# Opening of a four-layer graph network on one core: how bucket totals, walk tables, records and low weights are made

## What is computed

```python
edge_index = jnp.stack([src, dst])
x = _layernorm(x + _L0_gnn_ref(x, edge_attr_128, src, dst, L0_gnn_W0, ...), axis=-1)
x = _layernorm(x + _L1_gnn_ref(x, edge_index, L1_gnn_W1, ...), axis=-1)
x = _layernorm(x + _L2_gnn_ref(x, edge_index, L2_gnn_W1l, ...), axis=-1)
x = _layernorm(x + _L3_gnn_ref(x, edge_index, L3_gnn_W, L3_gnn_b), axis=-1)
```

```python
h = jnp.concatenate([n_embed[senders], n_embed[receivers]], axis=-1)
h = jnp.tanh(h @ W0 + b0)
h = jnp.tanh(h @ W1 + b1)
h = h @ W2 + b2
h = h * (e_embed @ Wg)
return _segment_mean(h, senders, n_embed.shape[0])
```

## Time and profile before

| | |
|---|---|
| runs | 3201.62, 3200.44, 3201.49 us; median 3201.49 |
| the profiled execution | 3200.9 us, its span 3199.2 us |
| busy, share of the span | PE 96%, weight loads 78%, VectorE 70%, ScalarE 49%, GpSimd 44% |
| opening | from 0 to about 106 us of the span |
| products of the totals (line 234) | 13 groups of 32 |
| 40 slices, granted clock | full in nearly all; 0.9 in the second |

### The profile page before, as it was taken

One profiled execution on the slowest core, in us unless ns is written; L12 is line 12 of the kernel. 1 busy time (PEld: TensorE's weight loads), 2 busy tenths in 40 slices (PEclk: granted clock), 3 DMA queues, 4 the chain that ended last, 5 costly groups with the idle time before them and its releaser, 6 DMA issues. The chain is left out here.

```text
span 3199.2 us, 65986 instructions
## 1 busy us (share of the span) xinstructions
PE 3084.0 (96%) x17656; PEld 2507.0 (78%) x17658; DVE 2244.3 (70%) x5604; ACT 1566.8 (49%) x3155; POOL 1395.0 (44%) x1479
## 2 busy tenths in 40 slices
PE   7699999999999999999998989999999999999899
PEld 6588888888888888888886777777777888887666
DVE  7688888888888888888886989995655222245532
ACT  2366666666666666666663777771111111001354
POOL 2577777777777777777773222220000000000111
PEclk9899999999999999999998999999999999999999
DMA  4555555555555555555554888887566777678475
GB/s 160 162 166 161 164 163 163 164 164 160 162 164 164 164 163 165 162 164 164 161 162 130 252 253 258 266 266 236 166 183 187 231 219 223 220 231 264 90 121 95
DMA packets 298303, 584.86 MB, mean 183 GB/s; under 512 B 43362, under 2 KB 150843, under 8 KB 298235
## 3 DMA queue, kind: packets, MB, share of 16 engines
q1 hardware_dynamic: 180960, 280.20, 29.5%
q0 software_dynamic: 90416, 254.46, 28.8%
q10 hardware_dynamic: 26858, 49.32, 4.2%
HBM read 493.97 MB, written 110.32 MB: 189 GB/s over the span
## 5 line engine op out<-in xcount | busy, mean ns | idle before, releaser
L967 PE MATMUL bank<-parts,ring 128*128 128x512 f32 x2500 | 622.8, 398 | 4.7 <-DVE T_buf L1739 2.6
L967 PEld LDWEIGHTS bank<-parts,ring 128*128 128x128 f32 x2500 | 461.0, 188 | 105.6 <-issue 5.7
L612 POOL DMA_INDIRECT msgs<-rows_out,sidx x416 | 409.1, 983 | 151.9 <-issue 95.1
L605 POOL DMA_INDIRECT p_in<-p_tab,gidx x416 | 404.6, 973 | 139.6 <-issue 122.7
L605 POOL DMA_INDIRECT q_in<-q_tab,gidx x416 | 399.0, 959 | 126.7 <-issue 125.2
L667 PE MATMUL bank<-hidden1h,w1h 128*108 128x512 f32 x936 | 407.1, 435 | 2.1 <-DVE hidden2l L855 2.1
L667 PE MATMUL bank<-w2h,hidden2h 108*128 108x256 f32 x1248 | 403.4, 323 | 0.0
L668 PE MATMUL bank<-hidden1l,w1h 128*108 128x512 f32 x936 | 369.0, 394 | 0.0
L669 PE MATMUL bank<-hidden1h,w1l 128*108 128x512 f32 x936 | 367.7, 393 | 0.0
L1123 PE MATMUL bank<-at_dst,at_src 128*128 128x320 f32 x1088 | 329.5, 384 | 36.3 <-DVE at_src L1083 29.1
L774 ACT ACTIVATE hidden2h<-bank,b1c 108x512 fp32r<-108x512 f32 (+1 forms) x312 | 214.8, 689 | 297.0 <-PE bank L683 297.0
(11 more groups left out here) (252 smaller groups left out, 6058.4 us busy)
## 6 DMA issues: line engine op xcount, KB each, us to landing
ring<-counts SPq DMA_DIRECT2D x500, 320.0 KB, 3.4
R_buf<-msgs SPq DMA_DIRECT2D x544, 130.0 KB, 3.1
counts<-cells ACTq DMA_DIRECT2D x125, 320.0 KB, 3.4
eT<-in_edge_T SPq DMA_DIRECT2D x104, 256.0 KB, 2.9
R_buf<-counts POOLq DMA_DIRECT2D x25, 480.0 KB, 5.2
R_buf<-counts POOLq DMA_DIRECT2D x25, 320.0 KB, 5.6
p_in<-p_tab,gidx POOLq DMA_INDIRECT x416, 3.2
q_in<-q_tab,gidx POOLq DMA_INDIRECT x416, 3.2
```

What stands on the lines that cost most here:

```text
L605: pool.indirect_dma_start(out=rows_in[:, z, c], out_offset=None, in_=tab[:], in_offset=bass.IndirectOffsetOnAxis(ap=gidx[:, z, which, c:c ...
L612: pool.indirect_dma_start(out=msgs[:], in_=rows_out[:, z, c], in_offset=None, out_offset=bass.IndirectOffsetOnAxis(ap=sidx[:, z, c:c + 1], ...
L967: mm = pe.matmul(bU[t].rearrange("p (w c) -> p w c", w=2), ring[:, cell(odd, a), t * P:(t + 1) * P].bitcast(dt), parts[k % 2][:, :, a].bit ...
```

## The change

Five edits, all in the opening.

1. **Totals over four chunks at once.** One product takes the one-hots of four chunks as its stationary side (4 x 25 = 100 columns) and those of the same four as its moving side (4 x 5 = 20). Of the 100 by 20 sums only the four 25 by 5 blocks of equal chunks are wanted; `found` and `spread` become 100 partitions high, and the identity that `spread` is multiplied by keeps only those blocks. The sum over partitions behind tile 17 reads 100 rows instead of 25.
2. **Walk tables from bf16.** `ended`, `jumpT` and `sign` are bf16, and `ones_b` takes the place of `ones_f`.
3. **Records piecewise.** The five instructions of `record()` stand singly behind `q_out` of tiles 5, 7, 9, 11 and 13.
4. **Low weights on GpSimd.** A third of `w1l` and of `w2l` each behind `xl` of tiles 8, 9 and 10.
5. The remainder of `w1h` stays on VectorE, behind `q_out` of tile 15.

```diff
@@ totals (PE) @@
-                            for c in range(OB):
-                                at = c % GC * B
-                                mm = pe.matmul(psum[7][0:T, at:at + B], oh_s[:, slot, c], oh_d[:, slot, c],
+                            for c in range(0, OB, GC):
+                                four = slice(c, c + GC)
+                                mm = pe.matmul(psum[7][0:GC * T, 0:GC * B],
+                                               oh_s[:, slot, four].rearrange("p c a -> p (c a)"),
+                                               oh_d[:, slot, four].rearrange("p c b -> p (c b)"),
                                                start=(n == 0 and slot == 0 and c == 0),
-                                               stop=(n == HN - 1 and slot >= 2 and c >= OB - GC),
+                                               stop=(n == HN - 1 and slot >= 2 and c == OB - GC),
@@ table (PE) and its operands @@
-                        lhs = [ones_f[0:BK - 1, :], jumpT[0:BK, 0:1], sign[0:BK - 1, 0:1]][what]
+                        lhs = [ones_b[0:BK - 1, :], jumpT[0:BK, 0:1], sign[0:BK - 1, 0:1]][what]
...
+                jumpT = ssb("jumpT", [P, P], BF16)
+                sign = ssb("sign", [P, 1], BF16)
+                ended = ssb("ended", [P, NST], BF16)
@@ sum over partitions (PE) @@
-                            pe.matmul(psum[6][:, 0:GC * BK], ones_f[0:T, :], spread[:].rearrange("p c a b -> p (c a b)"),
+                            pe.matmul(psum[6][:, 0:GC * BK], ones_f[0:GC * T, :], spread[:].rearrange("p c a b -> p (c a b)"),
@@ GpSimd @@
+                    def weights_low(k):
+
+                        pool.wait_ge(s_hi, 3)
+                        stand_alone(pool, s_up)
+                        pool.tensor_tensor(w1l[:, k].bitcast(F32R), w1[:, k], w1h[:, k], ALU.subtract)
+                        pool.tensor_tensor(w2l[:, k].bitcast(F32R), w2[:, k], w2h[:, k], ALU.subtract)
+
                     for n in range(T):
                         pool.wait_ge(s_xh, n + 1)
                         wait(pool, s_pq, n - 2)
                         pool.tensor_tensor(xl[:, n % 3].bitcast(F32R), xt[:, n % TB], xh[:, n % 3], ALU.subtract
                                            ).then_inc(s_xl, 1)
+                        if TB + 3 <= n < TB + 3 + H1F:
+                            weights_low(n - TB - 3)
@@ VectorE @@
-                    def record():
+                    def record(step):
...
+                        if step == 0:
+                            ch.note(v.tensor_copy(p_b[:], p_d))
+                        if step == 1:
+                            ch.note(v.tensor_copy(a_b[:], a_d))
+                        if step == 2:
+                            ch.note(v.scalar_tensor_tensor(flat_meta(1), bucket_f[:], float(P), p_s, ALU.mult, ALU.add))
+                        if step == 3:
+                            ch.note(v.scalar_tensor_tensor(local[:], a_d, float(P), p_d, ALU.mult, ALU.add))
+                        if step == 4:
+                            ch.settle()
+                            ch.note(v.scalar_tensor_tensor(flat_meta(2), block_f[:], -float(BW), local[:],
+                                                           ALU.mult, ALU.add))
...
-                        ch.link(v.tensor_copy(found[:].rearrange("p c b -> p (c b)"), psum[7][0:T, 0:GC * B]))
-                        shape = [T, GC, T, B]
+                        ch.link(v.tensor_copy(found[:].rearrange("p c b -> p (c b)"), psum[7][0:GC * T, 0:GC * B]))
+                        shape = [GC * T, GC, T, B]
                         v.tensor_tensor(spread[:], found[:].unsqueeze(2).broadcast_to(shape),
-                                        ident[0:T, 0:T].unsqueeze(1).unsqueeze(3).broadcast_to(shape), ALU.mult
+                                        ident[0:GC * T, 0:GC * T].rearrange("p (c a) -> p c a", c=GC).unsqueeze(3).broadcast_to(shape), ALU.mult
                                         ).then_inc(s_spread, 1)
...
-                        if n == HN - 3:
-                            record()
-                        if HN - 6 <= n < HN - 3:
-                            weights_low(n - HN + 6)
+                        if LATE < n < LATE + HN - 2 and (n - LATE) % 2 == 1:
+                            record((n - LATE) // 2)
+                        if n == LATE + HN - 2:
+                            mid = slice(H1R, 2 * H1R)
+                            v.wait_ge(s_hi, 3)
+                            v.tensor_tensor(w1h[mid, H1F].bitcast(F32R), w1[mid, H1F], w1h[mid, H1F], ALU.subtract)
```

More of the change, by code:

```diff
@@ L156, in build @@
                 src_b, block_b = (ssb(n, [P, G * GC], BF16) for n in ("src_b", "block_b"))
-                found = ssb("found", [T, GC, B])
-                spread = ssb("spread", [T, GC, T, B])
+                found = ssb("found", [GC * T, GC, B])
+                spread = ssb("spread", [GC * T, GC, T, B])
                 s_spread = ssem("s_spread")
@@ L174, in build @@
                 full_i = ssb("full_i", [P, BK], I32)
-                totT, stepsT, jumpT = (ssb(n, [P, P]) for n in ("totT", "stepsT", "jumpT"))
+                totT, stepsT = (ssb(n, [P, P]) for n in ("totT", "stepsT"))
+                jumpT = ssb("jumpT", [P, P], BF16)
                 endT = ssb("endT", [P, 1])
                 turned = ssb("turned", [P, 2])
-                sign = ssb("sign", [P, 1])
-                ended = ssb("ended", [P, NST])
+                sign = ssb("sign", [P, 1], BF16)
+                ended = ssb("ended", [P, NST], BF16)
                 row_f = ssb("row_f", [1, NST])
@@ L401, in _ @@
                     shifted(2)
-                    def record():
+                    def record(step):
                         flat_meta = lambda k: meta[:, :, k:k + 1].rearrange("p n o -> p (n o)")
-                        ch.note(v.tensor_copy(p_b[:], p_d))
-                        ch.note(v.tensor_copy(a_b[:], a_d))
-                        ch.note(v.scalar_tensor_tensor(flat_meta(1), bucket_f[:], float(P), p_s, ALU.mult, ALU.add))
-                        ch.link(v.scalar_tensor_tensor(local[:], a_d, float(P), p_d, ALU.mult, ALU.add))
-                        ch.note(v.scalar_tensor_tensor(flat_meta(2), block_f[:], -float(BW), local[:],
-                                                       ALU.mult, ALU.add))
+                        if step == 0:
[10 more added lines that the diff above has]
+                                                           ALU.mult, ALU.add))
@@ L420, in spread_out @@
                                         ).then_inc(s_spread, 1)
-                    def weights_low(step):
-                        v.wait_ge(s_hi, 3)
-                        mid = slice(H1R, 2 * H1R)
-                        if step == 0:
-                            v.tensor_tensor(w1l[:, 0:H1F].bitcast(F32R), w1[:, 0:H1F], w1h[:, 0:H1F], ALU.subtract)
-                        if step == 1:
-                            v.tensor_tensor(w1h[mid, H1F].bitcast(F32R), w1[mid, H1F], w1h[mid, H1F], ALU.subtract)
-                        if step == 2:
-                            v.tensor_tensor(w2l[:].bitcast(F32R), w2[:], w2h[:], ALU.subtract)
```

## The result

| | before | after |
|---|---|---|
| median of 15 runs, us | 3200.44 | 3193.38 |
| lowest to highest | 3197.19 to 3202.49 | 3187.74 to 3195.91 |
| the profiled execution; its span | 3200.9; 3199.2 | 3194.94; 3193.2 |
| first gather of the edge loop starts | 107.69 | 102.99 |
| first gather to the walk; walk; tail | 1631.1; 463.4; 997.0 | 1628.5; 462.8; 998.9 |

The walk is counted from its first product of the node sums to the first product of the stage behind it. Stretches at half clock are counted from the first group of totals on; the first products of the block, at about 15 us, run at half clock in every kernel.

What follows compares the result with a forecast made beforehand. PE was taken to bound the opening, the only part changed. Savings 6.5 + 4.0 + 1.1 less losses 1.5 and 1.2 gave 8.9 us: 3200.9 to 3192.0, plus 0.6 for the median, 3192.6 us; range 3188.5 to 3198.

Steps and rivals of the forecast that it cites:

- Totals: PE's 13 groups of bucket totals: 0.40 us each, 0.50 saved per group, 6.5 us in all (bounds 3.1 and 8.3).
- slow loads: Rival, chance 0.20: 100-column loads on PE take 77 ns, a group 0.66 us, totals save 3.1; kernel at 3194.9 us.
- Stalls removed: PE's waits for VectorE's one-hots: 2.32 us at record(), 1.50 of half clock, 0.22 behind low weights go; 4.0 us gained.
- I expect no fall: PE's clock in the opening stays full, because the largest new wait is short of 2.32 us.
- the prediction's own sign of being wrong: Forecast wrong if PE waits for xl, the clock falls in the opening, or the rest of the kernel changes length.
- Pieces of the record: Record pieces on VectorE behind tiles 5 to 13, w1h behind 15, overrun 0.45 us of slack per tile; 1.5 us lost.
- Low weights on GpSimd: Low weights on GpSimd in tiles 8 to 10 hold off VectorE: between 0 and 2.3 us lost, 1.2 taken.
- rival of the queue: Chance 0.04: xl queues behind low weights on GpSimd, held by one-hots, and PE waits 11.2 us; kernel at 3207.1 us.
- Tables: Table products on PE ahead of tile 24's end: bf16 makes two passes one; 1.1 us saved, bounds 0.8 to 1.5.
- Sum: The opening: 6.5 + 4.0 - 1.5 - 1.2 + 1.1 = 8.9 us saved.
- its last write: End of the opening: the last write to q_tab is issued some 9 us before 103.95.

Runs made afterwards that it cites:

- e1: The kernel before with the new totals alone, plus assertions on values loaded in the walk; first gather at 99.20 us, before 107.69.
- c1: The changed kernel itself, plus assertions on values loaded in the walk; first gather at 103.22 us, where the changed kernel without them had 102.99.
- e5: The changed kernel with assertions, each product of the totals loading 128 columns instead of 100; first gather at 99.76 us, 3.5 less than c1.
- c2: The changed kernel with assertions once more, run together with c0, b1 and b2; median 3247.79 us, first gather at 101.56.
- e7: The changed kernel with assertions, low weights on GpSimd moved behind its last xl; first gather at 98.28 us, 4.9 less than c1.
- e2: The changed kernel with assertions, w1l and w2l whole on VectorE behind q_out of tiles 8 and 10; first gather at 98.84 us, c1 103.22.
- e4: The changed kernel with assertions, walk tables and their ones in f32 again; first gather at 105.90 us, 2.7 more than c1.
- c0: The kernel before, plus assertions on values loaded in the walk; median 3250.36 us, first gather at 108.48.
- b1: The changed kernel with assertions and the edits of e5 and e7 together; median 3235.83 us, first gather at 96.41.
- e6: The changed kernel with assertions, one low-weight operation on GpSimd behind each xl of tiles 8 to 13; first gather at 98.35 us, c1 103.22.
- e3: The changed kernel with assertions, record() whole behind q_out of tile 10; first gather at 103.24 us, c1 103.22.
- b2: b1 with three pieces of the record and the w1h remainder moved behind the totals; median 3238.64 us, first gather at 94.86.

## Why the prediction was right, and where it was not

**Totals** ("I take 45 ns: 0.40 a group, 0.50 saved"): right, a little low. A group with a wait ahead cost 0.39 to 0.40, one without 0.35 to 0.36, and there the change-over from the tile ahead is 0.10 shorter too, so 0.50 in six tiles and up to 0.64 in seven, 7.4 us in sum; e1 gives 7.9 by its table row. The load was recorded with 138 ns (132 in c1), forecast about 130. The slow loads are refuted at full clock: a group of 0.66 (0.67) was seen only at half clock. What the step left out is the end of the totals: behind the last group VectorE's chain of bucket sums sets the time, and 0.70 us of the saving became waiting there (1.08 to 1.78).

By the Trainium skill (TensorE: Matmul & The Clock Gate, LDWEIGHTS) a load takes its columns over 1.2 ns, an estimate of 83 ns for 100; the runs show 45 ns a product with its load at full clock, so here the measurement decides. The fast load that the same page of the Trainium skill has (Weight-path perf modes), on for 128 columns that are not FP32, agrees with the runs: 26 ns a product with 128 in e5, 45 with 100.

**Stalls removed** ("4.0 us"): the 2.32 and the 0.22 went. The 1.50 of half clock did not: two stretches came elsewhere, one behind the wait before the first group (2.30) and one behind the 3.76. "I expect no fall" fails, by the prediction's own sign of being wrong. Its reason, the length of the longest wait, is too simple: the sum never named the first wait, and over all runs the length does not decide (2.79 without a fall in e1, 1.78 with one in c2).

**Pieces of the record** ("1.5 us lost"): 0.49 + 0.28 + 0.48 + 0.32 = 1.57; forecast were 0.84, 0.16, 0.45 and nothing for `w1h`. So the sum is right and its parts are not, the first meta column and `w1h` above all. The first meta column was read too long: it took 1.45 us before, beside an `xl` (53.09 to 53.95), and 0.90 here, the same as the second. `w1h` is what the text counted as fitting into the slack, and did not.

**Low weights on GpSimd** ("between 0 and 2.3 us over three tiles ... I take the middle, 1.2 us lost"): this is the step that failed. The waits at tiles 7 and 8 cost 3.76 in the profile after, 2.43 in c1 and 3.29 in c2; e7 and e2 put the whole at 2.7 to 4.9 with the clock. Two things in the step were wrong. It took GpSimd's operations as spread over three tiles, "beside 2.57 in which GpSimd waits"; but ScalarE, behind its rounding of W1 and W2, gives `xh` of tiles 8, 9 and 10 so close together (37.79, 39.05 and 41.76) that with low weights between them no pause is left, and most of the load falls on the one-hots ahead of one group. The trace of before had it: its `xl` of tiles 8 and 9 start at 37.99 and 39.35, with 0.63 us between them and not 2.57. And it took holding as a matter of one operation and another, a half microsecond each, whereas a row of GpSimd operations kept one `oh_s` waiting through four of them. The rival of the queue had the place right (GpSimd, tiles 8 to 10) and the direction wrong: the `w1l`, `w2l` and `xl` took 0.72 to 1.20, and `xl` was never late for PE. That one engine holds the other is read from the times alone: VectorE's long operations stand beside GpSimd's row, and go away with it in e2 and e7.

The Trainium skill (SBUF — State Buffer, Terms) says that the pair of ports is "held for the full instruction". For GpSimd the trace fits: `w2l` at 39.41 and `w1l` at 43.33 took 0.35 and 0.33 us more than their sisters, less than one VectorE operation each. For VectorE the wait went over four operations of GpSimd in a row.

**Tables** ("I take 1.1", bounds 0.8 to 1.5): 1.40 by the rows, 1.2 by e4.

**Sum.** Totals 7.4, tables 1.4, waits 2.54 to 5.33, one stretch more of 1.5: 7.4 + 1.4 - 2.8 - 1.5 = 4.5, less 0.7 of waiting behind tile 18, and 0.6 by which the first group happened to start earlier: 4.4, and the opening shows 4.7. The forecast's 8.9 was thus nearly twice too high for these two executions, and its last write, "some 9 us before 103.95", was issued 4.7 before. That the median still came out within 1 us of 3192.6 is in part luck: the openings of other pairs of executions gained 4.5 (before and c1) to 6.9 (c0 and c2), so the mean gain may lie above 4.7, but no pair gained 8.9; and the other stages were 1.3 us shorter in the profiled execution. The difference of the medians of 15 runs, 7.1 us, is what both together come to; how they share it in the runs without a profile is not known.

## What to carry to other kernels

When work is moved to an engine that can hold off the one on the critical path, as GpSimd does VectorE here, look at when the mover's own inputs arrive: if they come close together, the moved work makes one row of it, and all the holding falls on one place. Put such work where the held engine waits anyway (behind the last tile here: free, against waits of 2.4 to 3.8 us in the middle), or leave it where it is: on VectorE it cost some 0.4 us more than at the end. Count a saving on the critical engine only up to the next place where it waits for another: of the last group's 0.9 us of shorter work here 0.7 became waiting. And try a stationary side padded to 128 bf16 columns before one that is only as wide as needed: the 28 useless columns took 2.0 us of PE's work off 104 loads, of which 1.1 to 1.3 arrived (b1 against e7).

## What the runs showed of the hardware

- 128 bf16 columns load faster than 100: records of 96 to 98 ns against 126 to 138, and 26 ns a product against 45.
- A row of GpSimd operations without a pause kept a VectorE comparison with two operands in SBUF waiting 3.29 instead of 0.56 us. `q_out`, which reads PSUM, took 0.58 beside `w2l` (44.55 in the profile after), as alone.
- A wait on PE does not by itself tell whether the clock falls: behind 2.79 us (e1) and 1.43 (e6) it stayed at 1.00 up to 97 us; behind 2.32 in the kernel before it fell at once. The wait of 1.78 behind tile 18 stands in all twelve kernels with the new totals: in c1, c2, e3, e4, e7, b1 and b2 the clock fell within 1.6 us of it, in the other five not, and with 1.08 (before, c0) it did not either. The same kernel had one, two or three such stretches in its three profiled executions.
- An assertion on each value that the walk loads costs 50 us over the walk, 463.4 to 513.9.
